# Two layers of a graph network: 38 of 50 plain tiles by one-hots, and source keys that travel through DRAM to become broadcast rows

## The reference

```python
h = jnp.maximum(_layernorm(x, axis=-1), 0.0)
x = x + segment_sum((h * cj)[src], dst) * ci              # layer 0
h = jnp.maximum(_layernorm(x, axis=-1), 0.0)
x = x + (1 + eps) * h + segment_sum(relu(h[src] + edge_attr), dst)   # layer 1
```

## Time and profile before

| | us |
|---|---|
| median of 3 runs | 4817.13 (4811.87 to 4824.38) |
| the profiled execution | 4835.91 |
| its span | 4833.8 |
| PE busy | 3566.5 (74%) |
| DVE busy | 3722.4 (77%) |
| ACT busy | 3189.4 (66%) |
| POOL busy | 3598.8 (74%) |

### The profile page before, as it was taken

The page is one execution under the profiler, slowest core; times in us unless marked ns, Lnnn a source line. Parts: engine busy times, 40 slices in busy tenths (PEclk is TensorE's granted clock), DMA queues, the critical chain, the costliest instruction groups (busy, mean ns, idle before and its releaser), DMA issues.

```text
span 4833.8 us, 126665 instructions
## 1 busy us (share of the span) xinstructions
PE 3566.5 (74%) x42604; PEld 2785.6 (58%) x42604; DVE 3722.4 (77%) x11262; ACT 3189.4 (66%) x8706; POOL 3598.8 (74%) x3686
## 2 busy tenths in 40 slices
PE   0378878787878787878787888367777777777774
PEld 0256556565656565656565655356666666666664
DVE  9788878787878787878787876767677676777775
ACT  1367767676767676767676777366666666666664
POOL 6757777777777777777777777477777777777774
PEclk9999999999989999989998999678888888888887
DMA  6322222222222222222222221311211221211220
GB/s 110 62 52 54 57 54 54 54 57 54 54 54 57 54 54 54 57 54 54 54 57 54 54 54 29 87 39 53 57 44 52 57 57 54 57 49 47 57 57 26
DMA packets 442815, 265.39 MB, mean 55 GB/s; under 512 B 336196, under 2 KB 426804, under 8 KB 435704
## 3 DMA queue, kind: packets, MB, share of 16 engines
q1 hardware_dynamic: 322488, 187.55, 16.9%
q0 software_dynamic: 113888, 63.05, 6.9%
q10 hardware_dynamic: 5728, 5.82, 0.5%
HBM read 175.32 MB, written 80.85 MB: 53 GB/s over the span
## 4 chain that ended last, share of the span: by engine, by line
POOL 62%; issue 21%; DVE 4%; PE 3%; DMA 2%; ACT 1%; POOLq 0%; DVEq 0%; SPq 0%; ACTq 0%
POOL records L771 33%; POOL stage L759 22%; POOL message L752 7%; DVE arena L1753 1%; PE candidates L1247 1%; POOL message L759 1%; DVE arena L1729 1%; PE plain_ps L1259 1%; DMA stage<-in_edge_attr 1%; DMA stage<-table,src_plain 0%; PE sorted_agg L1187 0%; ACT message L987 0%; ACT centered L1039 0%; PE candidates L1170 0%; PE candidates L1165 0%
## 5 line engine op out<-in xcount | busy, mean ns | idle before, releaser
L771 POOL DMA_INDIRECT records<-stage,place_i x1875 | 1883.3, 1004 | 615.7 <-issue 591.8
L759 POOL DMA_INDIRECT stage<-table,src_plain x1250 | 1259.6, 1008 | 409.2 <-issue 377.8
L987 ACT ACTIVATE message<-candidates,member_is 128x96 bf16<-128x96 f32 x4080 | 1070.3, 397 | 355.1 <-PE candidates L1247 354.4
L1753 DVE TENSOR_SCALAR arena<-window_iota,dst_rel 128x224 bf16<-128x224 f16 (+1 forms) x4800 | 1079.9, 298 | 37.8
L880 ACT ACTIVATE arena<-key_rows 125x640 f16<-125x640 f16 x1000 | 652.0, 713 | 417.8 <-PE key_rows L1139 235.9
L1187 PE MATMUL sorted_agg<-arena 128*96 128x224 bf16 (+1 forms) x5000 | 655.1, 285 | 157.1 <-DVE arena L1753 110.2
L1139 PE MATMUL key_rows<-ident,record 128*125 128x128 f16 x5000 | 442.8, 242 | 421.2 <-DMA record<-records 272.8
L1729 DVE TENSOR_SCALAR arena<-arena,row_key 125x1280 bf16<-125x1280 f16 x1000 | 560.5, 560 | 249.6 <-ACT arena L880 222.1
L1139 PEld LDWEIGHTS key_rows<-ident,record 128*125 128x125 f16 x5000 | 398.8, 156 | 468.9 <-issue 340.1
L1187 PEld LDWEIGHTS sorted_agg<-arena 128*96 128x96 bf16 x5000 | 543.0, 137 | 181.7 <-issue 114.7
L1259 PE MATMUL plain_ps<-summed,message 128*96 128x224 bf16 x4080 | 540.6, 268 | 78.9 <-ACT message L987 76.4
(11 more groups left out here) (228 smaller groups left out, 5281.8 us busy)
## 6 DMA issues: line engine op xcount, KB each, us to landing
record<-records SPq DMA_DIRECT2D x50, 1650.0 KB, 7.3
stage<-in_edge_attr SPq DMA_DIRECT2D x125, 400.0 KB, 3.2
records<-pad SPq DMA_DIRECT2D x25, 1650.0 KB, 12.4
records<-stage,place_i POOLq DMA_INDIRECT x1875
stage<-table,src_plain POOLq DMA_INDIRECT x1250
message<-table,mid_src POOLq DMA_INDIRECT x384
xs<-in_x SPq DMA_DIRECT2D x8, 390.6 KB
table<-parts ACTq DMA_DIRECT2D x4, 585.9 KB
```

Source lines behind the costliest of these rows:

```text
L759: pool.indirect_dma_start(message[:, k, j, :] if l == 0 else rows[:, k, j, :], None, table0 if l == 0 else table1, bass.IndirectOffsetOnAx ...
L771: pool.indirect_dma_start(records, bass.IndirectOffsetOnAxis(ap=place_i[:, h, e:e + 1], axis=0), stage[:, h, e, :], None).then_inc(scatter ...
L987: last = nc.scalar.activation(direct_message[n % DB][:, m * WIDE:(m + 1) * WIDE], candidates[n % 2][:, m * WIDE:(m + 1) * WIDE], ACT.Copy, ...
L1753: last = nc.vector.tensor_scalar(dst_onehot(g, t), window_iota[:, 0:WA if tile == 0 else WT], dst_rel[:, h, tile:tile + 1], None, ALU.is_e ...
```

## The change

`SIDE` becomes 19: 38 of the plain tiles take the direct way, 12 are gathered. The cuts of each side are 5, 5, 5 and 4 tiles instead of 5, 4, 4 and 4.

The key rows of layer 0 no longer come from PE and ACT. One transpose (`turn_all`) turns the keys of all 100 tiles of a batch, 128 x 100 to 100 x 128; one ACT copy (`copy_turned`) brings them to `keys_turned`. SP stores these 100 rows to a DRAM array `turned`, waits for the store, and then reads each group back by one DMA in which the 1280 keys of the group are the source of all 125 partitions. Such a row has four rooms, two that were there and two in space that the middle tiles' one-hots leave free (`key_of`). DVE waits for the load instead of for ACT. Layer 1 keeps the old way. Two semaphores of the path for far destinations are merged into others to make room for the new ones, and a counter of GpSimd's gathers into that of its scatters.

The core of the diff:

```diff
-    SIDE = 17
+    SIDE = 19
-    CUTS = (0, 5, 9, 13, 17)
+    CUTS = (0, 5, 10, 15, 19)
...
+    turned = nc.dram_tensor("turned", (BATCHES, TILES * P), F16, kind="Internal").ap()
+    turned_t = turned.rearrange("b (t e) -> b t e", t=TILES)
+    turned_g = turned.rearrange("b (g e) -> (b g) e", g=GROUPS)
...
+        keys_turned = sb("keys_turned", [TILES, P], F16)
+        KEY_ROOMS = 4
+        more_rows = centered_room[0:NP, :].bitcast(F16)[:, 2 * C * F - 2 * GE:2 * C * F].rearrange("p (k e) -> p k e", k=2)
+        def key_of(l, g):
+            return more_rows[:, g % 2, :] if l == 0 and g % KEY_ROOMS >= 2 else key_row[:, g % 2, :]
...
                 load_record(0, b, 0)
                 if left >= 2:
                     load_stage(b + 2, h)
                     fill(b + 2, h)
+                if is_first(b):
+                    sp_at_least(parts_ready, CHUNKS)
+                sp.wait_ge(key_rows_copied[0], b + 1)
+                sp.sem_inc(loads_begun, 1)
+                sp.dma_start(turned_t[bass.ds(b, 1), :, :].rearrange("o t e -> (o t) e"), keys_turned[:]).then_inc(keys_stored, 16)
+                sp.wait_ge(keys_stored, 16 * (b + 1))
+                sp.sem_inc(loads_begun, 1)
+                for g in range(GROUPS):
+                    nth = GROUPS * b + g
+                    if g == 0:
+                        sp_at_least(src_onehot_ready[0], 2 * GROUPS * b)
+                    elif g >= KEY_ROOMS:
+                        sp_at_least(src_onehot_ready[0], 2 * (nth - KEY_ROOMS + 1))
+                    sp.dma_start(key_of(0, g), turned_g[bass.ds(nth, 1), :].to_broadcast([NP, GE])).then_inc(keys_loaded[g % KEY_ROOMS], 16)
...
+                def copy_turned(b):
+                    act.wait_ge(key_rows_ready[0], b + 1)
+                    at_least(act, keys_stored, 16 * b)
+                    nc.scalar.activation(keys_turned[:], key_rows[0][0:TILES, 0:P], ACT.Copy).then_inc(key_rows_copied[0], 1)
...
-                        if g + 3 < GROUPS:
-                            copy_keys(b, h, u, g + 3)
...
-                            if n in (DIRECTS - 3, DIRECTS - 2):
-                                copy_keys(*after(b, h, u), n - (DIRECTS - 3))
+                            if n == DIRECTS - 3:
+                                copy_turned(b + 1)
...
+                def turn_all(b):
+                    pe.wait_ge(record_loaded[0][0], 16 * (b + 1))
+                    at_least(pe, direct_copied_keys, SUBS * b)
+                    nc.tensor.transpose(key_rows[0][0:TILES, 0:P], record16[:, 0, :, 2 * F], ident16[:]).then_inc(key_rows_ready[0], 1)
...
-                    dve.wait_ge(key_rows_copied[l], 2 * nth + 2)
+                    if l == 0:
+                        uses = len(range(g % KEY_ROOMS, GROUPS, KEY_ROOMS))
+                        dve.wait_ge(keys_loaded[g % KEY_ROOMS], 16 * (uses * b + g // KEY_ROOMS + 1))
+                    else:
+                        dve.wait_ge(key_rows_copied[l], 2 * nth + 2)
```

More of the change, by code:

```diff
@@ L401, in gnn_two_layers @@
         key_rows_copied = per_layer("key_rows_copied")
+        keys_stored = sem("keys_stored")
+        keys_loaded = [sem(f"keys_loaded_{k}") for k in range(KEY_ROOMS)]
         src_onehot_ready = per_layer("src_onehot_ready")
@@ L632, in step0 @@
                     sp_at_least(direct_keyed, 1)
-                sp_at_least(key_rows_ready[0], 2 * GROUPS * b)
+                sp_at_least(key_rows_ready[0], b)
                 sp_at_least(dst_onehot_ready[0], GROUPS * b)
@@ L749, in gather_mid @@
             def gather_mid(h):
-                pool.sem_inc(gathers_begun, 1)
+                pool.sem_inc(scatters_begun, 1)
                 for j in range(MID):
@@ L1093, in _ @@
                         with act.Fori(0, UNITS) as s:
-                            act.wait_ge(far_sum, s + 1)
+                            act.wait_ge(far_sum, 2 * s + 1)
                             nc.scalar.activation(message[:, 0, :, 0:F], attr[:, 0, :, :], ACT.Relu).then_inc(far_first, 1)
-                            act.wait_ge(far_left, s + 1)
-                            nc.scalar.activation(message[:, 0, :, F:2 * F], attr[:, 0, :, :], ACT.Copy).then_inc(far_second, 1)
+                            act.wait_ge(far_sum, 2 * s + 2)
+                            nc.scalar.activation(message[:, 0, :, F:2 * F], attr[:, 0, :, :], ACT.Copy).then_inc(far_first, 1)
             for k in range(CHUNKS):
@@ L1222, in turn_direct_keys @@
                     if s < 2:
-                        pe.wait_ge(key_rows_copied[0], 2 * GROUPS * (b + 1))
+                        pe.wait_ge(key_rows_copied[0], b + 1)
                     else:
@@ L1318, in step0 @@
                                 mid_products(b)
-                            if n in (DIRECTS - 3, DIRECTS - 2):
-                                turn_keys(*after(b, h, u), n - (DIRECTS - 3))
+                            if n == DIRECTS - 3:
+                                turn_all(b + 1)
                         pick(*after(b, h, u), 0)
@@ L1986, in _ @@
                             nc.vector.tensor_tensor(attr[:, 0, :, :], attr[:, 0, :, :], rows[:, 0, :, :], ALU.add).then_inc(far_sum, 1)
[L1987 removed]
+                            dve.wait_ge(far_first, 2 * s + 1)
                             nc.vector.scalar_tensor_tensor(attr[:, 0, :, :], attr[:, 0, :, :], 0.0, message[:, 0, :, 0:F],
[L1989 to L1990 removed]
+                                                           ALU.max, ALU.subtract).then_inc(far_sum, 1)
+                            dve.wait_ge(far_first, 2 * s + 2)
                             nc.vector.tensor_tensor(message[:, 0, :, 2 * F:3 * F], attr[:, 0, :, :], message[:, 0, :, F:2 * F],
```

16 lines of the change are left out of this document (5 added, 11 removed).

## The result

The changed kernel takes 4971.84 us (median of 4 runs, 4971.75 to 4975.28), the kernel before beside it 4820.03: a ratio of 1.0321, 95% interval [1.0304, 1.0337], 152 us more. The forecast was 4915, with a range to 5005: the direction and the place of the loss (late key rows) held, the loss is half as large again as forecast, and the loop that carries it is the one the forecast put second. The profiled execution has a span of 4970.0 us.

A forecast was written before the change was run, and what follows sets the result against it. GpSimd was taken to pace layer 0 (238.2 us per pair of batches); late key rows make the two-batch loop 246.0. +7.8 over 11 pairs is +86, start +6, end +8: +100 on 4817, put at 4915, range 4820 to 5005.

The forecast's parts named there:

- Key rows at T + 30: Layer 0: first key row ready 30.0 us after T, the end of a batch's scatters, against T + 11.4 before.
- the store waits for the fill: SP's queue: the turned keys' store lands at T + 25.3, after the fill of a later batch's records, not T + 17.6.
- the two reasons given: Why the store does not pass the fill: both use the same queue, and the 16 engines are full (111%).
- the loop through GpSimd: Two batches of layer 0: scatters, key rows, VectorE's batch, ranks; 246.0 us per pair against 238.2, so +86 us.
- TensorE's loop: Layer 0, put second: direct stage, key transpose, copy, store, load, VectorE's one-hots; 120.1 us per batch, above 119.1.
- 102.5 + 9.5 = 112.0: TensorE's loop from VectorE's start to the key transpose: 102.5 us before, plus 9.5 for four more direct tiles.
- 1.5 + 1.9 + 4.6 = 8.0: TensorE's loop from key transpose to one-hot: transpose and copy 1.5 us, store 1.9, load 4.6.
- The sort's wait: SP's wait for the sort, once in four batches, comes closer to T; left in the range.
- Four gathers fewer: GpSimd, per batch: 5.2 us less, period 113.9; alone worth 114 us, if no other loop is longer.
- Transposes and copies removed: Main stage: TensorE loses 99 of 100 key transposes, ScalarE 19 of 20 copies, under VectorE's cover; costed at nothing.
- Start and tail: Layer 0's ends: +6 us where VectorE's first batch sets GpSimd's first wait, +8 us in the last gathers.
- The rule on engines: Key loads of 125 rows run on 5 of 16 engines; a load on all 16 makes a pair 3.3 us shorter.

The follow-up runs named there:

- fill17: The changed kernel with 34 direct tiles instead of 38, and SP issuing stage loads and fill behind the key loads: 4822 us, ratio 1.0005 to the kernel before.
- fill_act: The changed kernel with the fill issued by ScalarE on its own queue, ahead of its copy of the turned keys: 5080 us, ratio 1.0540 to the kernel before.
- keys17: The changed kernel with 34 direct tiles again, so the new key path alone: 4910 us, ratio 1.0187 to the kernel before.
- tiles19: The kernel before with 38 direct tiles and its old key path, so the tiles alone: 4800 us, ratio 0.9958 to the kernel before.
- tiles18: The kernel before with 36 direct tiles and its old key path: 4801 us, ratio 0.9960 to the kernel before.
- fill18: The changed kernel with 36 direct tiles, and stage loads and fill issued behind the key loads: 4820 us, ratio 1.0000 to the kernel before.

## Why the prediction was right, and where its sum was short

- **Key rows at T + 30: right in two batches of four.** There the key load leaves at T + 24.8 to 26.4 (25.4 forecast), the first one-hot is at T + 30.5 to 32.4, and the second group's 2.6 to 2.9 us later (2.7 forecast). In the batch that waits for the sort the first one-hot is at T + 43 to 46, and in the one behind it, where TensorE itself turns late, at T + 36 to 37: 36.0 on average over batches 3 to 22. That the store waits for the fill was the right choice, and fill17 shows that stage loads and fill together are nearly all of the key path's cost. Of the two reasons given, the shared queue is not needed; the full engines fit what fill_act shows.
- **Which loop: wrong order.** The sum was made with the loop through GpSimd (123.0 per batch) and put TensorE's second (120.1). Measured is TensorE's, at 126.3, and no scatter of layer 0 is on the chain. keys17 shows the other loop as a part of the bound where TensorE has 9.5 us more room, so both are real and close. That the forecast came this close is in part luck: with the prediction's own 120.1 for the loop that bounds, its sum would be 4817 + 22 x 1.0 + 14 = 4853, a quarter of the loss.
- **TensorE's loop, the mis-sized term.** Its 102.5 + 9.5 = 112.0 from one-hot to turn is measured as 111.2 to 112.3 in three of the four batches shown. Its 1.5 + 1.9 + 4.6 = 8.0 from turn to one-hot is 13.3 on average there: the sum gave the fill to the other loop alone, and the load is 6.0 rather than 4.6. The rest is VectorE's loop turn, which lengthens the stretch by 5 to 6 us once in four batches. The granted clock is no part of it: in the direct stage it is 1.00 (2.4 GHz) in after too (1616 to 1671 us, TensorE busy 52.23 of 55), as in the earlier trace rows. In the main stage it is 0.86 instead of 0.93 (1585 to 1609 us, TensorE busy 16.44 of 24 instead of 20.09), and there VectorE, busy 21.97 of 24, is the bound.
- **The sort's wait**, left in the range without a price: it holds SP until T + 14 to 17.5 once in four batches. Taken away alone it gives 21 us.
- **Four gathers fewer:** right that they count only if no other loop is longer. tiles19 gains 20 of the 114.
- **Transposes and copies removed** at no gain: no run put a price on this by itself. In keys17, with the same 34 tiles, the stretch from first one-hot to the next turn is 103.6 to 106.3 us in the batches 3 to 21 that are without VectorE's loop turn, no shorter than the 102.5 of before.
- **Start and tail:** the scatters of batch 2 begin 4.8 us earlier (307.5 after 312.3) (+6 forecast), and the last gathers take 17.6 us more (+8 forecast). Layer 0 ends 152.5 us later than before (3241.8 and 3089.3), which is the result: 139 us of it lie in the 22 batches in between.
- **The rule on engines**, weighed in the prediction as 3.3 us per pair, is 2.3 per batch in the period and 55 us in all, since it shortens TensorE's loop in every batch.

Open: what keeps tiles18 and fill18 above GpSimd's period. In fill18 three of four intervals between the ends of scatters are 116 to 119 us and the fourth is 125 to 126; it follows the batches in which VectorE turns its loop and SP waits for the sort, and no run parts these two. In tiles18 nearly every second interval is long (120 to 123 us, the others 115 to 118), in step with TensorE's loop of two batches, and scatters are on its chain.

## What to carry to other kernels

A DMA round trip put into a loop can cost what was issued ahead of it (here 9.4 us instead of 2.5): look for the large transfers issued shortly before it, on any queue, and move them behind it, before the work it replaces is counted as saved. Price a new wait in every loop that it joins, not only in the one that bounds the kernel now; delays that cover each other show little when only one is taken away. Then choose the split of the work (here 36 direct tiles, not 38) so that the engine that is relieved still sets the pace.

## What the runs showed of the hardware

A store of 25 KB from SP took 1.5 to 2.8 us with no fill in flight, until the load behind it left, and 8.1 us where it was issued 1.4 us behind a fill of 1650 KB on another queue. A load of 125 rows held 31.6% of the 16 engines, one of 128 rows 62.3%, and the time to first use fell from 6.0 to 3.9 us for 2.4% more bytes. Three stage loads took SP 10.5 us to issue right behind the record load, with no wait in the program between them.
